# A two-layer decoder on one core: half of the tokens of its first expert layer go through sorted expert blocks

## The reference

```python
def _L0_xattn_ref(hidden_states, token_ids, Wg, Wu, Wd):   # Wg = Wu = Wd = ctx_2048, (4, 256, 256)
    E = 4; VOCAB = 12500
    tid = jnp.clip(token_ids, 0, VOCAB - 1)
    expert_ids = jnp.minimum(tid // (VOCAB // E), E - 1)
    out = jnp.zeros_like(hidden_states)
    for e in range(E):
        g = jax.nn.silu(jnp.einsum('bsd,fd->bsf', hidden_states, Wg[e]))
        u = jnp.einsum('bsd,fd->bsf', hidden_states, Wu[e])
        y = jnp.einsum('bsf,df->bsd', g * u, Wd[e])
        out = jnp.where((expert_ids == e)[..., None], y, out)
    return out
...
x = _layernorm(x + _L0_xattn_ref(x, itok_BxS_13_99985, ctx_2048, ctx_2048, ctx_2048), axis=-1)
```

## Time and profile before

| | us |
|---|---|
| device time, median of 3 runs | 430.19 (429.94 to 431.14) |
| profiled execution: span from first to last instruction | 429.5 |
| PE busy in the span | 413.5 (96%) |
| DVE, ACT, POOL busy | 255.2, 241.6, 270.6 |
| mean granted clock of PE | 0.997 of full speed |

### The profile page before, as it was taken

One profiled execution on the slowest core, in us unless ns is written; L12 is line 12 of the kernel. 1 busy time (PEld: TensorE's weight loads), 2 busy tenths in 40 slices (PEclk: granted clock), 3 DMA queues, 4 the chain that ended last, 5 costly groups with the idle time before them and its releaser, 6 DMA issues.

```text
span 429.5 us, 9350 instructions
## 1 busy us (share of the span) xinstructions
PE 413.5 (96%) x3645; PEld 361.4 (84%) x3645; DVE 255.2 (59%) x637; ACT 241.6 (56%) x423; POOL 270.6 (63%) x237
## 2 busy tenths in 40 slices
PE   8999999999999999899999999999699999999994
PEld 7888999988889888788888899798578989888983
DVE  4778657748536338966654588655455676343243
ACT  4848654764484775352734767573526757554543
POOL 1744454564798577674876548457647386877763
PEclk9999999999999999999999999999999999999998
DMA  8644000021233313042222103121523332565402
GB/s 256 195 149 145 3 2 0 2 76 50 73 91 123 103 53 124 24 127 96 79 86 76 38 0 111 51 88 63 167 74 96 118 103 78 151 165 151 141 33 98
DMA packets 19623, 39.29 MB, mean 91 GB/s; under 512 B 2763, under 2 KB 7371, under 8 KB 19580
## 3 DMA queue, kind: packets, MB, share of 16 engines
q1 hardware_dynamic: 19004, 38.17, 28.8%
q10 hardware_dynamic: 576, 0.53, 0.4%
HBM read 37.08 MB, written 1.08 MB: 89 GB/s over the span
## 4 chain that ended last, share of the span: by engine, by line
PE 75%; DVE 10%; issue 4%; ACT 4%; DMA 3%; SPq 2%; POOL 1%; POOLq 0%; DVEq 0%; ACTq 0%
PE bank L492 13%; PE bank L493 13%; PE bank L495 13%; PE bank L762 8%; PE bank L764 7%; PE bank L763 7%; PE bank L842 2%; DMA pk_raw<-w_attn_dram 2%; PE bank L781 2%; PE bank L830 1%; DVE q_buf L1584 1%; DMA brow<-cw_dram 1%; PE bank L515 1%; PE bank L812 1%; PE bank L813 1%
## 5 line engine op out<-in xcount | busy, mean ns | idle before, releaser
L1307 POOL TENSOR_TENSOR h_lo<-hraw,h_hi 128x512 fp32r<-128x512 f32 x76 | 98.1, 1294 | 77.3 <-ACT h_hi L1097 77.2
L492 PE MATMUL bank<-xT_hi,pk_hi 128*128 128x512 f32 x256 | 102.9, 402 | 1.1 <-DVE hraw L1625 1.1
L493 PE MATMUL bank<-xT_hi,pk_lo 128*128 128x512 f32 x256 | 101.0, 395 | 0.0
L1097 ACT ACTIVATE h_hi<-hraw 128x512 fp32r<-128x512 f32 x76 | 47.8, 629 | 72.3 <-DVE hraw L1625 70.3
L1625 DVE TENSOR_TENSOR hraw<-bank,sil 128x512 f32<-128x512 f32 x76 | 52.4, 689 | 54.6 <-ACT sil L1085 24.6
L495 PE MATMUL bank<-xT_lo,pk_hi 128*128 128x512 f32 x256 | 80.4, 395 | 0.0
L762 PE MATMUL bank<-pk_hi,h_hi 128*128 128x256 f32 x272 | 77.8, 286 | 0.2 <-issue 0.2
L764 PE MATMUL bank<-pk_hi,h_lo 128*128 128x256 f32 x272 | 76.9, 283 | 0.0
L763 PE MATMUL bank<-pk_lo,h_hi 128*128 128x256 f32 x272 | 76.8, 282 | 0.0
L1313 POOL TENSOR_TENSOR pk_lo<-pk_raw,pk_hi 128x512 fp32r<-128x512 f32 (+1 forms) x44 | 74.8, 1700 | 2.8 <-ACT pk_hi L1115 2.6
L492 PEld LDWEIGHTS bank<-xT_hi,pk_hi 128*128 128x128 f32 x256 | 48.2, 188 | 11.8 <-DVE hraw L1625 1.6
(11 more groups left out here) (256 smaller groups left out, 736.6 us busy)
## 6 DMA issues: line engine op xcount, KB each, us to landing
pk_raw<-pk_f_dram SPq DMA_DIRECT2D x28, 384.0 KB, 3.3
pk_raw<-pk_f_dram SPq DMA_DIRECT2D x16, 512.0 KB, 3.5
pk_raw<-pk_f_dram SPq DMA_DIRECT2D x16, 256.0 KB, 3.3
kv_buf<-pk_x_dram SPq DMA_DIRECT2D x4, 512.0 KB, 3.7
x_tok<-x_rows_dram SPq DMA_DIRECT2D x1, 1024.0 KB, 9.5
pk_raw<-pk_x_dram SPq DMA_DIRECT2D x4, 256.0 KB, 6.2
brow<-cw_dram SPq DMA_DIRECT2D x4, 256.0 KB, 3.4
cw_late<-cw_dram SPq DMA_DIRECT2D x4, 256.0 KB, 4.0
```

Of the source, the lines that this page charges most:

```text
L492: pe.matmul(o, w(kc)[0], x(kc)[0], start=kc == 0, stop=False)
L493: pe.matmul(o, w(kc)[1], x(kc)[0], start=False, stop=False)
L1097: A(h_hi[:, row, at * 512:(at + 1) * 512], hraw[:, s % 2, :], ACT.Copy).then_inc(sems["hid_hi"], 1)
L1307: pool.tensor_tensor(h_lo[:, row, q], hraw[:, s % 2, :], h_hi[:, row, q].bitcast(F32), ALU.subtract).then_inc(sems["hid_lo"], 1)
```

## The change

The four dense units of half 1 go (units 4 to 7, slots 8 to 15); golden slots are 8 to 39 now. In their place the tokens of half 1 are sorted by expert:

- DVE makes `route0` at the start (`k0`, before in `first_constants`). PE counts with five small matmuls each token's rank within its expert (`x0_rank`), and DVE works out a slot number per token, with every expert's run beginning at a multiple of 128, and which expert owns each of the NB = 7 blocks of 128 slots (`x0_slots`, steps k1 to k4).
- POOL sends the normalised rows of tiles 4 to 7 to their slots in DRAM by four indirect DMAs (P0 to P3); SP loads the sorted rows back (`x0_load`, L1).
- Seven blocks then run, whatever the counts are: PE transposes the block (stage 0), multiplies it with its expert's matrix (stage 1, 6 matmuls of 256 columns, the matrix addressed through a register), transposes the hidden rows (stage 2), and makes the down product (stage 3, 6 matmuls). ACT copies and silus and DVE's remainders and product stand between. `x1.13` is stage 1 of block 3.
- SP stores the results (Y0 to Y6), POOL fetches them back into token order by four indirect DMAs (Q0 to Q3), and DVE adds them (`x1.50` to `x1.53`).
- The four experts' packs lie together in `xp_hi`/`xp_lo`, so the golden weights' ring is free from the start: G1 and D1 are made earlier. The norm of half 0 behind the first MoE (`r0.1`) is applied by POOL, not ACT, and its statistics stand between the blocks (`x1.40` to `x1.43`). The transposes of half 1 (`n1.2`) go.

```diff
-g20 u20 g21 u21 g22 u22 d9 g23 u23 d10 g24 u24 g25 u25 r1.2 d11 r1.3 d12 g26 u26 g27 u27 g28 u28 g29 d13 u29 g30 u30
+g3 d0 g4 g5 g6 d1 g7 d2 x1.00 x1.01 d3 x1.10 x1.02 x1.11 x1.03 x1.20 x1.12 x1.04 x1.21 x1.30 x1.13 x1.05 x1.22 x1.31
+x1.14 x1.06 x1.23 x1.32 x1.15 x1.24 x1.33 x1.16 x1.25 x1.34 x1.26 x1.35 r0.2 x1.36 g8 r0.3 u8 g9 u9 g10 u10 g11 d4 u11
...
+NB = HT + EX - 1
+U_F0, U_F1 = EX, EX + 2 * E0
 S_F0, S_F1 = 2 * U_F0, 2 * U_F1
...
-        aT_hi = (h_hi[:, 0, :], xp_hi[:, 1, :])
-        aT_lo = (h_lo[:, 0, :], xp_lo[:, 1, :])
+        aT_hi = (h_hi[:, 0, :], pk_hi[:, 0:1024])
+        aT_lo = (h_lo[:, 0, :], pk_lo[:, 0:1024])
+        ew_hi = xp_hi[:, :, :].rearrange("p a w -> p (a w)")
+        ew_lo = xp_lo[:, :, :].rearrange("p a w -> p (a w)")
...
+            sp.wait_ge(sems["ones_ready"], 1)
+            sp.dma_start(xs_dram.rearrange("(j p) d -> p j d", p=P),
+                         zero_r[:, 0:D].bitcast(F32).unsqueeze(1).to_broadcast([P, NB, D])
+                         ).then_inc(sems["x0_zero"], 16)
+
+            def x0_load():
+
+                sp.wait_ge(sems["x0_sent"], 16 * HT)
+                rows = xs_dram.rearrange("(j p) d -> p j d", p=P)
+                to = x_sent[:, 0:NB * D].rearrange("p (j d) -> p j d", d=D)
+                sp.dma_start(to[:, 0:2, :], rows[:, 0:2, :]).then_inc(sems["x0_in0"], 16)
+                sp.dma_start(to[:, 2:NB, :], rows[:, 2:NB, :]).then_inc(sems["x0_in1"], 16)
+
+            def x0_store(j):
+
+                sp.wait_ge(sems["x0_y"], j + 1)
+                sp.dma_start(ys_dram[j * P:(j + 1) * P, :], y_sent[:, j * D:(j + 1) * D]
+                             ).then_inc(sems["x0_ys"], 16)
...
+            def x0_rank():
+
+                pe.wait_ge(sems["rank_in"], 2)
+                ranks = bank[7][:, 0:(HT + 1) * EX]
+                pe.matmul(ranks, tri_m, tab[:, 0:(HT + 1) * EX], start=True, stop=False, skip_group_check=True)
+                for t in range(1, HT + 1):
+                    m = pe.matmul(ranks[:, t * EX:], ones_m, tab[:, 0:(HT + 1 - t) * EX], start=False, stop=t == HT,
+                                  skip_group_check=True)
+                m.then_inc(sems["rank_ps"], 1)
+
+            block_of = [None]
+
+            def x0_expert(stage, j):
+
+                if stage == 0:
+                    if j == 0:
+                        pe.wait_ge(sems["x0_in0"], 16)
+                    elif j == 2:
+                        pe.wait_ge(sems["x0_in1"], 16)
+                    for c in range(KC):
+                        a = j * D + c * P
+                        m = pe.transpose(x0_bank(0, j)[:, c * P:(c + 1) * P], x_sent[:, a:a + P], ident)
+                    m.then_inc(sems["x0_t_ps"], 1)
+                elif stage == 1:
+                    if j == 0:
+                        pe.wait_ge(sems["a0_res"], 4)
+                        pe.wait_ge(sems["blocks_ready"], 1)
+                        block_of[0] = pe.value_load(block_w[0:1, 0:1], min_val=0, max_val=EX ** NB - 1)
+                    else:
+                        pe.wait_ge(sems["x0_mul"], max(j - 1, 1))
+                    x0_product(x0_bank(1, j), j, x0_cols, xT_hi, xT_lo, "x0_xh", "x0_xl").then_inc(sems["x0_g_ps"], 1)
+                elif stage == 2:
+                    if j < 2:
+                        pe.wait_ge(sems["hid_mul"], S_F0 - 1 + j)
+                    pe.wait_ge(sems["x0_mul"], j + 1)
+                    for c in range(KC):
+                        m = pe.transpose(x0_bank(2, j)[:, c * P:(c + 1) * P], hraw[:, j % 2, c * P:(c + 1) * P], ident)
+                    m.then_inc(sems["x0_v_ps"], 1)
+                else:
+                    if j < 2:
+                        pe.wait_ge(sems["acc_done"], 4 * EX - 2 + 2 * j)
+                    else:
+                        pe.wait_ge(sems["x0_y"], j - 1)
+                    x0_product(x0_bank(3, j), j, h0_cols, h_hi, h_lo, "x0_hh", "x0_hl").then_inc(sems["x0_d_ps"], 1)
+
+            def x0_product(o, j, cols, hi, lo, hi_done, lo_done):
+
+                at = ((block_of[0] >> (2 * j)) & (EX - 1)) * W_X0
+                pe.wait_ge(sems[hi_done], j + 1)
+                for c in range(KC):
+                    w = bass.ds(at + c * D, D)
+                    pe.matmul(o, cols(hi, j)[:, c, :], ew_hi[:, w], start=c == 0, stop=False)
+                    pe.matmul(o, cols(hi, j)[:, c, :], ew_lo[:, w], start=False, stop=False)
+                pe.wait_ge(sems[lo_done], j + 1)
+                for c in range(KC):
+                    m = pe.matmul(o, cols(lo, j)[:, c, :], ew_hi[:, bass.ds(at + c * D, D)], start=False, stop=c == KC - 1)
+                return m
...
+            def x0_send(t):
+
+                if t == 0:
+                    pool.wait_ge(sems["x0_zero"], 16)
+                    pool.wait_ge(sems["slots_ready"], 1)
+                pool.wait_ge(sems["ln_done"], 4 * nth(1) + t + 1)
+                pool.indirect_dma_start(xs_dram, bass.IndirectOffsetOnAxis(ap=slot_i[:, t:t + 1], axis=0),
+                                        x_tok[:, HT + t, :], None).then_inc(sems["x0_sent"], 16)
+
+            def x0_fetch(t):
+
+                pool.wait_ge(sems["x0_ys"], 16 * NB)
+                pool.indirect_dma_start(o_tok[:, t, :], None, ys_dram,
+                                        bass.IndirectOffsetOnAxis(ap=slot_i[:, t:t + 1], axis=0)
+                                        ).then_inc(sems[f"x0_got{t // 2}"], 16)
+
+            def norm_apply(n):
+                pool.wait_ge(sems["ln_rstd"], halves_before(n) + 1)
+                for t in range(HT):
+                    T = HT * (n % 2) + t
+                    pool.tensor_scalar(x_tok[:, T, :], x_tok[:, T, :], rstd[:, T:T + 1], shift[:, T:T + 1], ALU.mult,
+                                       ALU.add).then_inc(sems["ln_done"], 1)
...
+            def x0_slots(i):
+
+                if i == 1:
+                    dve.wait_ge(sems["rank_ps"], 1)
+                    dve.tensor_copy(tab[:, 32:32 + (HT + 1) * EX], bank[7][:, 0:(HT + 1) * EX]
+                                    ).then_inc(sems["rank_read"], 1)
+                    dve.memset(begins[:, 0:1], 0.0)
+                elif i == 2:
+                    dve.wait_ge(sems["rank_read"], 1)
+                    link(STT(over, iota8[:, 0:HT].unsqueeze(1).to_broadcast([P, EX, HT]), float(P),
+                             count.unsqueeze(2).to_broadcast([P, EX, HT]), ALU.mult, ALU.is_lt))
+                    link(dve.tensor_reduce(blocks, over, axis=AXX, op=ALU.add))
...
+                elif i == 3:
+                    link(STT(at, begins.unsqueeze(1).to_broadcast([P, HT, EX]), float(P),
+                             rank.rearrange("p (t e) -> p t e", e=EX), ALU.mult, ALU.add))
...
+                    dve.tensor_copy(slot_i[:, :], slot_f).then_inc(sems["slots_ready"], 1)
+                else:
+                    link(TT(last, begins.unsqueeze(1).to_broadcast([P, NB, EX]),
+                            iota8[:, 0:NB].unsqueeze(2).to_broadcast([P, NB, EX]), ALU.is_le))
...
+                    TS(block_w[:, :], owners, -float((EX ** NB - 1) // (EX - 1)), None, ALU.add
+                       ).then_inc(sems["blocks_ready"], 1)
+
+            def x0_expert(stage, j):
+
+                if stage == 0:
+                    dve.wait_ge(sems["x0_xh"], j + 1)
+                    TT(x0_cols(xT_lo, j), x0_bank(0, j).rearrange("p (c t) -> p c t", c=KC),
+                       x0_cols(xT_hi, j).bitcast(F32), ALU.subtract).then_inc(sems["x0_xl"], 1)
+                elif stage == 1:
+                    dve.wait_ge(sems["x0_silu"], j + 1)
+                    if j < 2:
+                        dve.wait_ge(sems["hid_lo"], S_F0 - 1 + j)
+                    else:
+                        dve.wait_ge(sems["x0_v_ps"], j - 1)
+                    TT(hraw[:, j % 2, 0:D], x0_bank(1, j), sil[:, j % 2, 0:D], ALU.mult).then_inc(sems["x0_mul"], 1)
+                elif stage == 2:
+                    dve.wait_ge(sems["x0_hh"], j + 1)
+                    TT(h0_cols(h_lo, j), x0_bank(2, j).rearrange("p (c t) -> p c t", c=KC),
+                       h0_cols(h_hi, j).bitcast(F32), ALU.subtract).then_inc(sems["x0_hl"], 1)
+                elif stage == 4:
+                    dve.wait_ge(sems["acc_done"], 4 * (EX - 1) + j + 1)
+                    link(dve.bn_stats(stats[:, j, :], x_tok[:, j, :]))
+                else:
+                    T = HT + j
+                    dve.wait_ge(sems[f"x0_got{j // 2}"], 32)
+                    TT(x_tok[:, T, :], x_tok[:, T, :], o_tok[:, j, :], ALU.add).then_inc(sems["x0_added"], 1)
+                    dve.wait_ge(sems["x0_added"], j + 1)
+                    link(dve.bn_stats(stats[:, j, :], x_tok[:, T, :]))
...
                 if kind == "f0" and i == 1:
-                    act.wait_ge(sems["out_ready"], out_no(EX + 1))
+                    act.wait_ge(sems["a0_o_ps"], 4)
```

251 lines of the change are left out of this document (175 added, 76 removed).

## The result

The changed kernel took 437.15 us (median of 4; 435.25 to 441.92), the kernel before 430.47 beside it (median of 4; 429.94 to 431.14): a ratio of 1.0133 with a 95% interval of 1.0099 to 1.0166. It is slower by some 6 us. The prediction said 430.8 and held everything up to 435.3 possible. The profiled execution is the longest of the four, with a span of 440.2 us; the others spanned 433.1 to 436.5. What follows from it is checked against the profiles of e1 and e10.

A forecast was written before the change was run, and what follows sets the result against it. PE, busy 96% of the span, was taken as the bound up to layer 1's opening norm. Its work falls 10.5 us, waits and other costs bring the sum to +0.6, so 430.8 us was forecast, range 426.9 to 435.3.

The forecast's parts named there:

- the count: Before the attention products: PE's five rank matmuls and DVE's copy of their result, +0.35 us.
- sorting: Before the first block: PE waits for rows sent by POOL's indirect DMAs and loaded back, +1.2 us.
- registers: At the blocks: PE's load of `block_w`, 0.7, and 43 register instructions, 1.3; together +2.0 us.
- inside the blocks: Block 1's gate waits for block 0's silu and product; later blocks wait for nothing; +0.75 us.
- norm of half 0: Behind the last blocks: the norm, hidden before behind half 1's gates, is no longer fully covered; +1.5 us.
- golden downs: In the golden MoE: PE waits before d4, d8 and d11 of 2.0, 1.35 and 1.65 us; +5.0 us.
- router of half 1, d7: PE's waits before half 1's router and down product d7: the prediction has no term for them.
- clock: Rival in the blocks: PE at 1.2 GHz doubles their 13.1 us, giving 443.9 us; chance 0.02.
- the second rival: POOL becomes the bound through indirect DMAs of 2 us each, at first block and before D4; 435.7 us; chance 0.18.
- The register rival: PE's sequencer is the bound in the blocks, 5.2 + 2.1 us in place of 2.0; 436.1 us; chance 0.13.
- contention, +0.3, mostly off PE's path: DVE's four additions of fetched rows stretched beside a busy POOL, up to 1.5 us each; +0.3 us.

The follow-up runs named there:

- e1: The changed kernel run again with no edit; 438.93 us, ratio 1.021 to the kernel before.
- e10: The changed kernel with slot 16's product moved ahead of the third addition of fetched rows in DVE's list; 439.19 us, ratio 1.0194 to the kernel before.
- e8: The changed kernel with fixed experts for the blocks, without the loaded word and PE's register instructions; 442.83 us, ratio 1.022 to the kernel before.
- e13: e10 with 12, 6 and 8 products of zeros before d4, d8 and d11, in an unread bank; 431.26 us, ratio 1.0018 to the kernel before.
- e6: The changed kernel with POOL's four indirect fetches replaced by plain DMAs on SP, rows left in slot order; 438.82 us, ratio 1.0142 to the kernel before.
- e3: The changed kernel with only the order of steps on POOL and ACT altered; 435.68 us, ratio 1.0123 to the kernel before.
- e4: The kernel before with PE's list altered: dense d7 ahead of g17, golden d8 directly behind u17; 438.91 us, ratio 1.0176 to the kernel before.
- e9: e4 with 20 products of zeros ahead of d8; 434.19 us, ratio 1.0054 to the kernel before.
- e17: e13 with two more products of zeros before half 1's router and three before the transposes opening layer 1; 431.76 us, ratio 1.0023 to the kernel before.
- e14: e13 with as many products of 32 rows by 17 columns in place of the zeros; 434.79 us, ratio 1.0044 to the kernel before.
- e15: The kernel before with 26 products of 32 rows by 17 columns before the down products of units 8, 12 and 15; 430.18 us, ratio 0.9963.

## Why the prediction was wrong, step by step

Places are those of the changed kernel's profile. The stretch runs from PE's first gate to the first gate of golden half 1.

| step of the prediction | forecast | shown | from |
|---|---|---|---|
| the count | +0.35 | +0.4, not clear of the spread | first gate at 40.48 to 41.82 (mean 40.92) in thirteen profiles with the change, 39.69 to 41.83 (40.55) in five without |
| sorting | +1.2 | +0.8, and elsewhere | waits before g6 and d2; none before the blocks |
| registers | +2.0 | +0.3 | e8; no row of before had a small load, the 2.1 us of the earlier trace rows is a transfer of 256 KB |
| inside the blocks | +0.75 | +0.7 | wait before block 1 |
| norm of half 0 | +1.5 | +0.3 | 8 transposes in 1.18 us for 0.87 |
| golden downs | +5.0 | +7.3 | waits of 3.06, 2.87, 1.39 |
| router of half 1, d7 | 0 | +0.8 | 0.59, 0.23 |
| clock | 0 | +3.8 to 4.6 | e10 against e13; d4, d8 and the products behind the router of half 1 in part at the lower level |

**Right.** The seven blocks for four dense units: PE's own work falls by 10.3 us, forecast 10.5. The first golden gate stands at 83.86 against 84 to 86; that it comes so close is in part luck, with sorting, registers and norm priced too dear and 1.2 us of short gaps not priced. A send on POOL took 0.96 to 1.19 us, where 1.0 was taken. The Trainium skill's page "SBUF — State Buffer" (section "SBUF: two separate sides") has the descriptors of such sends held up while DVE holds the port that both share; none of the eight indirect DMAs of this trace took over 1.19 us, so no run here shows it. The row quoted for it, 1.67 us, shows the other direction, DVE held beside POOL. POOL's three fetches are not what makes d8 late (e6), so the second rival fell. The register rival fell with e8; the Trainium skill's page "DMA: Bandwidth & Descriptors" (section "Latency and other measured facts") has some 600 ns for a `tensor_load`, and the whole of the register work cost half of that on PE's path here.

**Mis-sized.** d4 waits 3.06 us instead of 2.0: the chain left out one table load of ACT, 1.28 us, though the earlier trace rows has one ahead of a silu in the same place of the kernel before. d8 waits 2.87 instead of 1.35, for two reasons. The chain took DVE to be free for the product of slot 17, which stands behind the norm's statistics and two additions in DVE's list; and "contention, +0.3, mostly off PE's path" was too small. The earlier trace rows showed a DVE operation stretched to 1.67 us beside POOL, and "up to 1.5 each" was read from it. It should have been as long as POOL's longest product there, 3.5 us; that addition out of the way is worth 0.64 us before d8 (e10). The same section of the Trainium skill's page "SBUF — State Buffer" says as much: a DVE operation with two inputs in SBUF and a POOL operation that reads SBUF lock each other out for the whole instruction. The trace agrees for the addition: 126.76 against 126.47 us. The operation on 4 columns in e3 (103.35 against 103.33 us) has one input in SBUF, so this part of the rule does not cover it. The section was cited for POOL's descriptors and not for DVE's additions, which are the operations that the change adds.

**Failed: the clock, put at nothing.** It was given two chances in a hundred, and only as a rival in which the blocks run slowly. The argument, "1.00 in the window where PE is busy 8.85 of 10 us", was a share over ten microseconds with a single wait of 1.13 us in it. From its first gate to 170 us the kernel before has no wait of 0.3 us, so it could not show what one of 3 us does. The forecast itself named three waits of 2.0, 1.35 and 1.65 us and did not ask what PE's clock does behind them. In the changed kernel's profile the matmuls at the lower level take 4.6 us longer than at the upper in this stretch, and e13, whose waits are filled, is 3.8 us shorter there than e10. The Trainium skill's page "TensorE: Matmul & The Clock Gate" (section "What's actually happening") was quoted for it, that activity releases the throttle. Its other half, that the lower level is what an idle PE falls back to, is the one that bore on this change; e4 against e9 agrees with it, while the fall behind the router of half 1 in e17 comes without a wait.

**How far the clock alone explains the miss.** e13, without low clock, took 431.26 us and e14, with low clock behind both waits in its profile, 434.79; both are inside the range that ends at 435.3. But e13 has none of the pauses of the section on the late stall, e14 has 2.3 us of them, the kernel before 4.0 (2.53 and 1.46) and the changed kernel 3.8 (1.19 and 2.57). These pauses are not a cost of the change, and they flatter e13. Set beside e15, which has no pause either, e13's ratio to the kernel before is 0.0055 higher, about 2.4 us; the forecast stretch at full clock says the same, 125.1 us against 122.5. That is what the change costs without low clock, where +0.6 was forecast. The clock adds some 4 us in the stretch.

**The whole stretch, counted.** From the first gate to the first gate of golden half 1 the changed kernel takes 129.5 us and the kernel before 122.5, 7.0 more. In both traces the distance from each matmul's start to the next can be split into the usual distance of its line and what goes beyond. The usual distances fall from 122.1 to 111.8 us (-10.3). Gaps of 0.15 us or more beyond them are 11.9 us against 0.2 (+11.7), the matmuls in the low stretches take 4.6 longer (+4.6), and shorter gaps are 1.2 against 0.2 (+1.0). The waits shown in the table add up to 10.2 and not 11.7, because a shown wait starts at the modelled end of the last product, some 0.16 us behind the place where the next could have started, and the smallest are not in it. The other 2.7 us of the profiled difference arise behind 170 us, where the changed kernel has low clock in 220 to 230 and 315 to 325 us and the kernel before has none until its last slice.

## What to carry to other kernels

Where PE never waits, the first wait that a change puts in can cost more than its length: in these kernels a wait of 3 to 5 us was often followed by a stretch at the lower clock, 1.5 us more at d4 and d8 of the changed kernel and 2.8 behind e4's wait. Price each forecast wait with that, and test it by products of zeros into a free bank, which cost next to nothing while PE would stand idle. Such a test adds instructions too: run it with tiny products beside it, as e14, before the whole gain is put down to the clock. Removing work that was independent of the other engines' chains (here the dense units between router and golden slots) removes cover: list what each freed stretch was hiding, and price small DVE operations with two SBUF inputs by POOL's longest instruction that can stand beside them. And profile the same program twice before explaining a difference of 1%: a pause at a fixed product and a clock that varies behind it were each a good part of the effect.

## What the runs showed of the hardware that was not expected

- PE stands still for 2.0 to 2.7 us at one fixed product in a run of 128 products of 32 rows by 17 columns, 0.01 us apart. It goes on 1.23 to 1.53 us after a 16384-byte packet of its instruction queue has ended, in all 30 pauses of 0.5 us or more. Twenty to thirty products more on PE, 150 to 200 us earlier, shorten it or take it away; e8, with fewer instructions, has three.
- 12 products of 32 rows by 17 columns did not keep the clock up through a wait of 3 us (0.73 behind it in e14's profile), 12 of 512 columns did (1.00 in e13).
- The clock also fell behind 16 products of 16 columns with no wait before them (0.74 in 155 to 160 us of e17).
- A DVE operation on 4 columns took 2.09 us, and ended within 0.02 us of POOL's product beside it.
- The spread did not go with the stall: without it, e9's nine executions lie within 2.4 us (433.62 to 435.96), at clocks of 0.993 to 0.998, but e15's twelve within 5.4 (427.73 to 433.10), at 0.991 to 0.999.
